# Convolution and attention on one core: queries of the last chunks on GpSimd, scores folded ahead of their copy, an earlier load of x

## The reference

```python
xf = x.reshape(b, c, n)
q = jnp.einsum('oc,bcn->bon', Wq, xf) + bq[None, :, None]      # 32 x 4096
k = jnp.einsum('oc,bcn->bon', Wk, xf) + bk[None, :, None]      # 32 x 4096
v = jnp.einsum('oc,bcn->bon', Wv, xf) + bv[None, :, None]      # 256 x 4096
att = jnp.einsum('bdi,bdj->bij', q, k) / jnp.sqrt(d_k)
att = jax.nn.softmax(att, axis=-1)
out = jnp.einsum('bcj,bij->bci', v, att).reshape(b, c, h, w)
cat = jnp.concatenate([gamma * out, x], axis=1)
fused = jnp.einsum('oc,bchw->bohw', Wf, cat) + bf[None, :, None, None]
```

## Time and profile before

| | us |
|---|---|
| median of 3 executions | 1976.79 (1976.61 to 1981.90) |
| the profiled execution, whole | 1979.12 |
| its span, first to last instruction | 1977.3 |
| TensorE busy | 1951.3 |
| VectorE, ScalarE, GpSimd busy | 1686.4, 1712.1, 1393.9 |
| mean granted clock of TensorE | 0.995 |

### The profile page before, as it was taken

The page is one execution under the profiler, slowest core; times in us unless marked ns, Lnnn a source line. Parts: engine busy times, 40 slices in busy tenths (PEclk is TensorE's granted clock), DMA queues, the critical chain, the costliest instruction groups (busy, mean ns, idle before and its releaser), DMA issues.

```text
span 1977.3 us, 46381 instructions
## 1 busy us (share of the span) xinstructions
PE 1951.3 (99%) x15656; PEld 1920.5 (97%) x15656; DVE 1686.4 (85%) x2713; ACT 1712.1 (87%) x2282; POOL 1393.9 (70%) x669
## 2 busy tenths in 40 slices
PE   9999999999999999999999999999999999999999
PEld 8899999999889999999988999999998899999998
DVE  7888888887788889988688888899868888888896
ACT  7799999997779999999778999999978899999996
POOL 3577777778457777777746777777765677777775
PEclk9999999999999999999999999999999999999999
DMA  4211111110321111111042111111104111111111
GB/s 147 80 19 19 18 21 21 21 18 16 123 72 23 17 17 20 21 21 22 12 129 67 23 22 16 18 19 21 22 12 134 38 23 22 21 16 17 20 22 17
DMA packets 297816, 69.70 MB, mean 35 GB/s; under 512 B 280528, under 2 KB 281296, under 8 KB 297680
## 3 DMA queue, kind: packets, MB, share of 16 engines
q1 hardware_dynamic: 296864, 67.90, 15.9%
q10 hardware_dynamic: 816, 0.13, 0.0%
HBM read 34.41 MB, written 33.55 MB: 34 GB/s over the span
## 4 chain that ended last, share of the span: by engine, by line
PE 93%; DVE 3%; issue 1%; DMA 1%; ACT 1%; SPq 1%; POOL 0%; DVEq 0%; ACTq 0%; POOLq 0%
PE ps_o L417 75%; PE ps_s L409 11%; PE ps_p L284 3%; PE ps_o L284 3%; PE ps_s L301 1%; DMA xf<-x 1%; DVE top L649 1%; PE ps_p L319 1%; PE ps_p L315 1%; SPq L154 1%; DVE kq_rest L749 0%; DVE kq_rest L742 0%; DVE keys L746 0%; ACT keys L507 0%; DVE lo L636 0%
## 5 line engine op out<-in xcount | busy, mean ns | idle before, releaser
L842 POOL TENSOR_TENSOR raw<-raw,top_m 128x1024 f32<-128x1024 f32 x508 | 1208.8, 2413 | 281.5 <-DVE top_m L684 244.4
L695 DVE TENSOR_TENSOR lo<-ps_p,hi 128x1024 fp32r<-128x1024 f32 x512 | 622.6, 1216 | 166.9 <-ACT ps_p L578 160.9
L649 DVE TENSOR_TENSOR top<-ps_s,top 128x512 f32<-128x512 f32 x960 | 658.5, 686 | 60.1 <-ACT raw L495 10.5
L417 PE MATMUL ps_o<-val_hi,hi 128*128 128x258 f32 x4096 | 663.7, 284 | 12.7 <-DVE val_lo L759 12.7
L571 ACT ACTIVATE hi<-raw 128x1024 fp32r<-128x1024 f32 x508 | 539.6, 1062 | 153.7 <-PE ps_o L417 143.3
L417 PE MATMUL ps_o<-val_lo,hi 128*128 128x256 f32 x4096 | 656.6, 282 | 0.0
L417 PE MATMUL ps_o<-val_hi,lo 128*128 128x258 f32 x4096 | 600.2, 284 | 0.0
L417 PEld LDWEIGHTS ps_o<-val_hi,hi 128*128 128x128 f32 x4096 | 566.7, 190 | 14.4 <-DVE val_lo L759 10.7
L495 ACT ACTIVATE raw<-ps_s 128x512 f32<-128x512 f32 x1024 | 552.7, 592 | 30.2 <-PE ps_s L409 2.7
L417 PEld LDWEIGHTS ps_o<-val_lo,hi 128*128 128x128 f32 x4096 | 563.7, 190 | 0.0
L417 PEld LDWEIGHTS ps_o<-val_hi,lo 128*128 128x128 f32 x4096 | 540.7, 191 | 0.0
(11 more groups left out here) (69 smaller groups left out, 1076.6 us busy)
## 6 DMA issues: line engine op xcount, KB each, us to landing
xf<-x SPq DMA_DIRECT2D x32, 512.0 KB, 3.9
conv_d<-conv_st SPq DMA_DIRECT2D x64, 256.0 KB, 2.0
result<-conv_d SPq DMA_DIRECT2D x512, 32.0 KB, 1.8
out<-result SPq DMA_DIRECT2D x510, 32.0 KB, 1.6
raw<-wf2T SPq DMA_DIRECT2D x1, 256.0 KB, 3.6
raw<-wv SPq DMA_DIRECT2D x1, 256.0 KB, 4.1
raw<-wf1T SPq DMA_DIRECT2D x1, 256.0 KB, 4.6
raw<-wkqT ACTq DMA_DIRECT2D x1, 64.0 KB, 2.6
```

What stands on the lines that cost most here:

```text
L417: last = nc.tensor.matmul(ps_o[:, i, 0:width], p[:, t % 2, jl * I + i * P:jl * I + (i + 1) * P], v[:, j, 0:width], start=opens and jl == 0 ...
L649: nc.vector.tensor_tensor(top[:, new], scores, top[:, new if half else old], ALU.max).then_inc(max_done, 1)
L695: nc.vector.tensor_tensor(lo[:, t % 2], ps_p[:].rearrange("p h n -> p (h n)"), hi[:, t % 2].bitcast(F32), ALU.subtract).then_inc(lo_done, 1)
L842: nc.gpsimd.tensor_tensor(raw[:, slot], raw[:, slot], top_m[:, r].unsqueeze(1).broadcast_to((P, JQ, I)), ALU.subtract).then_inc(sub_done, 1)
```

## The change

In chunks 6 and 7 (`LATE` is 6) the queries no longer go through VectorE. ScalarE copies rows 64 to 127 of `ps_p` with the bias, unrounded, into a new tile `q_raw` (the bias of rows 96 to 127 is set to zero for that); GpSimd rounds the queries out of it, copies them, and makes their rest with two operations of two inputs. Subtracting the split of x's chunk 7 goes from GpSimd to VectorE. TensorE waits for `q_raw` in place of the finished queries before it writes `ps_p[:, 0]` again, and for the queries themselves only in stage 2 of block 0.

For chunk 7's scores the order of ScalarE and VectorE is turned round: VectorE folds as soon as TensorE has written, and ScalarE copies once the fold is counted; ScalarE takes the second convolution of chunk 6 ahead of these copies. TensorE and GpSimd get a wait each for these copies in the first block, since the fold's count no longer implies the copy. In stage 0 of block 0 `scores_ahead` comes before `lead_first`.

The load of chunk 2 of the next image goes from the projection's start to just before the stores of the last block, behind a wait for the split of chunk 0.

```diff
@@ SyncE
-                    if c + 2 < CHUNKS:
+                    if c + 2 < CHUNKS and (c > 0 or first):
                         sp.wait_ge(x_split, b * CHUNKS + (c + 1))
                         load_x(b, c + 2)
                     store_conv(b, c)
@@ SyncE, attend_image
                 for n in range(BLOCKS):
+                    if not last_image and n == BLOCKS - 1:
+                        sp.wait_ge(x_split, b * CHUNKS + (CHUNKS + 1))
+                        load_x(b + 1, 2)
@@ TensorE, project
-                    pe.wait_ge(q_out, C + 1)
-                    pe.wait_ge(q_copied, C + 1)
+                    pe.wait_ge(q_raw_done, b * (CHUNKS - LATE) + (CHUNKS - LATE))
                     convolve(ps_p[:, 0], 0)
...
                 if c == CHUNKS - 2:
-                    pe.wait_ge(q_out, C + 1)
+                    pe.wait_ge(k_out, C + 1)
+                    pe.wait_ge(q_raw_done, b * (CHUNKS - LATE) + 1)
                     project_kq(c + 1, C + 1)
@@ TensorE, attend
                     a = t + AHEAD
+                    if first and t == 1:
+                        pe.wait_ge(raw_done, H + 2 * (a - 1))
...
+                    if first and t == 2:
+                        pe.wait_ge(q_out, b * CHUNKS + CHUNKS)
+                        pe.wait_ge(q_copied, b * CHUNKS + CHUNKS)
                     if first and t == 0:
+                        scores_ahead(t)
                         lead_first()
-                        scores_ahead(t)
@@ ScalarE
-                    act.wait_ge(s_ready, base + (2 * made + half + 1))
+                    act.wait_ge(max_done if folded else s_ready, base + (2 * made + half + 1))
...
-                    nc.scalar.activation(queries[2 * CK:R3, span(c)], ps_p[2 * CK:R3, 0], ACT.Identity,
-                                         bias=bkkqq[2 * CK:R3]).then_inc(q_hi_done, 1)
+                    if c < LATE:
+                        nc.scalar.activation(queries[2 * CK:R3, span(c)], ps_p[2 * CK:R3, 0], ACT.Identity,
+                                             bias=bkkqq[2 * CK:R3]).then_inc(q_hi_done, 1)
+                    else:
+                        act.wait_ge(q_out, C)
+                        nc.scalar.activation(q_raw[2 * CK:P], ps_p[2 * CK:P, 0], ACT.Identity,
+                                             bias=bkkqq[2 * CK:P]).then_inc(q_raw_done, 1)
...
                 if last_chunk:
+                    conv_out(ps_p[:, 1], 1, C - 1)
                     early_scores(c)
-                    conv_out(ps_p[:, 1], 1, C - 1)
@@ VectorE
-                    dve.wait_ge(raw_done, base + (h + 1))
+                    dve.wait_ge(s_ready if at_once else raw_done, base + (h + 1))
...
+                    if c >= LATE:
+                        return
+                    if c == 0 and not first:
+                        dve.wait_ge(q_out, C)
...
                 kq_lo(c, C)
+                if c == CHUNKS - 2:
+                    split_x(C + 1, c + 1)
@@ GpSimd, project
-                if c > 0:
+                if c == CHUNKS - 1:
+                    pool.wait_ge(q_out, C)
+                elif c > 0:
                     pool.wait_ge(x_split, C + 1)
...
+                    L = snap(pool, b * (CHUNKS - LATE) + (c - LATE))
+                    pool.wait_ge(k_copied, C + 1)
+                    pool.wait_ge(q_raw_done, L + 1)
+                    pool.sem_inc(kq_seen, 1)
+                    nc.gpsimd.tensor_copy(queries[2 * CK:R3, span(c)], q_raw[2 * CK:R3]).then_inc(q_rounded, 1)
+                    pool.wait_ge(q_rounded, L + 1)
+                    pool.sem_inc(kq_seen, 1)
+                    nc.gpsimd.tensor_copy(queries[0:CK, span(c)], queries[2 * CK:R3, span(c)]).then_inc(q_copied, 1)
+                    pool.wait_ge(q_copied, C + 1)
+                    pool.wait_ge(q_out, C)
+                    nc.gpsimd.tensor_tensor(kq_rest[R3:P], q_raw[2 * CK:R3], queries[2 * CK:R3, span(c)].bitcast(F32),
+                                            ALU.subtract).then_inc(q_rest_done, 1)
+                    pool.wait_ge(q_rest_done, C + 1)
+                    nc.gpsimd.tensor_tensor(queries[CK:2 * CK, span(c)], q_raw[R3:P], kq_rest[R3:P],
+                                            ALU.add).then_inc(q_out, 1)
@@ GpSimd, attend
+                    if t == QUADS - 3 and isinstance(n, int) and n == 0:
+                        pool.wait_ge(raw_done, b * HALVES + 2 * AHEAD)
```

More of the change, by code:

```diff
@@ L213, in store_last, with project_image @@
                         store_piece(sp, b, n, i, g)
-            def project_image(b):
+            def project_image(b, first):
                 for c in range(CHUNKS):
-                    if c + 2 < CHUNKS:
+                    if c + 2 < CHUNKS and (c > 0 or first):
                         sp.wait_ge(x_split, b * CHUNKS + (c + 1))
@@ L617, in spread_bkq @@
                 dve.wait_ge(vec_loaded, 16)
-                for g, u in enumerate((0, 0, 1, 1)):
-                    last = nc.vector.tensor_copy(bkkqq[g * CK:(g + 1) * CK], bkq[u * CK:(u + 1) * CK])
+                nc.vector.memset(bkkqq[R3:P], 0.0)
+                nc.vector.tensor_copy(bkkqq[0:CK], bkq[0:CK])
+                last = nc.vector.tensor_copy(bkkqq[2 * CK:R3], bkq[CK:2 * CK])
                 last.then_inc(bkq_spread, 1)
@@ L637, in split_x, with fold_scores @@
                                         ALU.subtract).then_inc(x_split, 1)
-            def fold_scores(base, made, old, new, halves=(0, 1)):
+            def fold_scores(base, made, old, new, halves=(0, 1), at_once=False):
                 for half in halves:
@@ L864, in project @@
                 nc.gpsimd.tensor_copy(keys[CK:2 * CK, span(c)], keys[0:CK, span(c)]).then_inc(k_copied, 1)
-                pool.wait_ge(q_hi_done, C + 1)
-                pool.wait_ge(k_copied, C + 1)
-                pool.sem_inc(kq_seen, 1)
-                nc.gpsimd.tensor_copy(queries[0:CK, span(c)], queries[2 * CK:R3, span(c)]).then_inc(q_copied, 1)
-                if c < CHUNKS - 1:
+                if c < LATE:
+                    pool.wait_ge(q_hi_done, b * LATE + (c + 1))
+                    pool.wait_ge(k_copied, C + 1)
+                    pool.sem_inc(kq_seen, 1)
+                    nc.gpsimd.tensor_copy(queries[0:CK, span(c)], queries[2 * CK:R3, span(c)]).then_inc(q_copied, 1)
                     pool.wait_ge(q_copied, C + 1)
```

22 lines of the change are left out of this document (15 added, 7 removed).

## The result

| | before | after |
|---|---|---|
| median | 1976.61 us (5 executions) | 1968.11 us (5, 1967.36 to 1968.25) |
| the profiled execution | 1979.12 | 1968.11 |
| its span | 1977.3 | 1966.3 |
| mean granted clock | 0.995 | 0.997 |

The ratio of the mean times is 0.9951, with an interval of 0.9936 to 0.9965; by the medians the change makes the kernel 8.5 us faster. Forecast were 1957 us and a range of 1953.5 to 1967.0; the time is 1.1 us outside the range, and the gain less than half of the 20 us forecast. So the question of this part is where the rest of the expected gain went.

The account below looks back on a forecast made before the run. TensorE was busy 99% of the span, so only its stands and slow-clock time could give: 17.1 us at the heads plus 3.0 for the load, 20.1, less 0.3 for the port, off 1976.79 gives 1957 us; range 1953.5 to 1967.0.

Parts of the forecast that it names:

- So at 1.3 us GpSimd costs nothing: Chunks 6 and 7: GpSimd's two-input operations take 1.3 us each and delay nothing; from 1.7 us they would.
- the chain: Start of chunk 7's projection to start of `lead_first`: forecast to shorten by 7.2 us over four images.
- rival E: Shared port: GpSimd work beside VectorE's two-input operations; a doubled split costs 3.2 us, 1960 us; chance 0.05.
- I take the clock as held: Head of the attention: TensorE stands 1.2 us instead of 3.13, so the clock stays at 1.00.
- rival A: Head of the attention: the clock falls anyway, total gain 14.3 us, 1962.5 us; chance 0.12.
- rival D: Stages 1 to 3: ScalarE and VectorE can't keep up at full clock, 1 us per image, 1961 us; chance 0.12.
- The load: x's chunk 2 loaded earlier: TensorE's projection wait goes in three images, taken as 3.0 us together.
- Folding ahead of the copy: Chunk 7: VectorE folds before ScalarE copies; costed at nothing, between a gain and a loss of 0.5 us.
- Stage 0 at the full clock: First stage of the attention: 24 matmuls, 2.9 us, plus a wait for `lo`, 3.4 us.
- The queries off the chain: Chunk 7: VectorE's 1.5 us of query work between the keys' rest and the folds goes.
- rival B: GpSimd sets the pace and the kernel is slower; 1984 us at 4 us per two-input operation; chance 0.04.
- C: Rival: the load gives nothing, as another input of chunk 1 is as late; 1960 us; chance 0.10.

Follow-up runs that it names:

- e2: The changed kernel with two more waits on GpSimd, keeping its two-input operations off VectorE's split and first maximum; 1967.75 us.
- e3: The changed kernel with a second buffer for raw queries, and GpSimd's copy of chunk 7's keys ahead of chunk 6's two operations; 1966.72 us.
- e11: e3 with chunk 7's two GpSimd operations put off behind the head, to stage 4 of block 0; 1964.48 us.
- e5: The changed kernel with GpSimd making only chunk 7's queries; chunk 6's stay on VectorE and chunk 7's split on GpSimd; 1965.10 us.
- e10: e5 with one more wait: GpSimd's stage 5 subtraction in block 0 starts only behind the second block's maximum; 1965.47 us.
- e4: The changed kernel with 12 unneeded score matmuls filling TensorE's stand ahead of `lead_first`; 1966.86 us.
- e6: The changed kernel with ScalarE's copies of chunk 7's scores ahead of the folds again and its last convolution's order put back; 1968.18 us.
- e1: The kernel before the change with only the earlier load of x's chunk 2; 1974.06 us.

## Why the prediction was wrong

The direction was right, with every part of the change doing what it says. The sum was 20.1 us against the profiled execution and 11.0 came. Three steps failed, and the baseline.

1. **"So at 1.3 us GpSimd costs nothing", and the folds from 554.85.** This is the step with the largest miss: the chain gained 2.3 us and not 7.2. The size of an operation by itself was right (1.28 to 1.29 us measured, 1.3 taken). What was wrong was to let it run beside VectorE: the first took 2.16 us, so chunk 6's queries were ready 2.72 us behind the start of the projection (547.87 to 550.59), where the forecast has 1.88 (551.47 to 553.35). ScalarE waited 0.95 us for them, the copy of the keys came behind them, and the folds began 4.10 us behind the projection, not 3.38 (0.72 lost). Then the maximum stood 0.58 us for GpSimd. Together 1.3 us per image, 5.2 in four; the table is short by 4.9. That was rival E, which I had given 0.05 and priced for the split only. Its evidence was read wrongly. The mean of 64 maxima, 435 ns against 420, was taken for the price of lying beside GpSimd. In that trace no maximum takes more than 0.49 us; those of 0.46 to 0.49 start when a subtraction of GpSimd has only 0.2 us left. The 15 ns are the price of such tails and say nothing about a maximum that starts with 0.7 us of the other's instruction left, as in after. e2 (the same operations at other times: 1719 to 1288 ns) and e3 (a copy of 0.16 us at 1.15) show the exclusion, e11 shows the chain without it (11.6 us). It also bears out what the Trainium skill says, in the page "SBUF — State Buffer", section "SBUF: two separate sides": the pair of ports that VectorE and GpSimd share is an exclusive lock, held for the whole instruction, and the other fully blocks. The traces agree in each meeting (2.16, 1.00 and 1.15 us above), but for 0.12 to 0.14 us: by that rule each would have been priced at the remainder of the other's instruction, 1.00, 0.71 and 1.13 us, where 0.88, 0.58 and 0.99 were lost.

2. **"I take the clock as held."** It fell in three of four images, at stands of 1.70, 1.66 and 2.17 us, and held in image 0 at one of 2.23. That was rival A, 0.12. Stage 0 gained 5.2 us and not 8.5. The stand was longer than the 1.2 us of the forecast mainly because of step 1 (the chain), so this miss is half a child of the first: in the profiled executions of e5 and e11, with a shorter chain, the clock held in all four images, in that of e10, with e5's chain, in three. But the rule used, that the length of the stand decides, is itself not one (last section).

3. **Nothing behind the head gives way (rival D, 0.12).** e4 holds the clock and gets 1.3 us for 3.6; e5, e10 and e11 gain 11.8 to 14.1 us up to stage 1 and keep 0.9 to 1.9 in the rest, where runs with a slow head keep 3.3 to 4.9. In after it is image 0, whose clock held, that gives 1.0 us back, as much as the whole shortfall of the rest. D looked for the loss in stages 1 to 3, in ScalarE and VectorE at their own pace. It came in stages 6 and 7 of the first block, and what was late there was VectorE, held up in the second block's maximum by GpSimd (the table under e4): step 1 once more, in a place that the prediction didn't look at. ScalarE's own pace is not it: it needs 2.85 us per stage (its exponentials start at 562.13 and 565.00 in e5) against TensorE's 3.36, and in image 1 of e4 and of e5 it has already waited 0.2 us for TensorE, twice, before it waits for VectorE. No run takes this meeting away altogether with the clock held in all images; where it is absent by chance (images 1 and 2 of e5), 0.2 us is lost, with a wait for `hi`.

4. **The baseline.** I took the sum made against a profiled execution of 1979.12 us off the median of 1976.79, 2.3 us below. But what the change removes here is in part time at the slow clock, of which that execution may have had more than the median one; after's profiled execution is at its median (1968.11), and the profiled gain is 11.0 us where the medians give 8.5. Taken off the profiled execution my own sum gives 1959.3, as the prediction said in brackets. The later runs of before bear that out: of 28 executions those with a mean granted clock of 0.996 to 0.998 took 1975.4 to 1978.5 us, those with 0.992 to 0.994 took 1979.2 to 1981.7. A median of before hangs on how many of each it has; against the 1979.68 us of one such set e6, as fast as after, is 11.5 us faster. So part of the shortfall against 20 us, 2 to 3 us of it, is luck of the executions and none of the mechanism.

5. **What held.** The load: forecast 3.0, measured 3.9 in e1 in the three stretches that it bears on, all three waits gone. Folding ahead of the copy: forecast at nothing, measured at 0.07 us. Stage 0 at the full clock: forecast 3.4, measured 3.41 in image 0 and 3.2 to 3.4 in e4. The queries off the chain: the step of 1.5 us per image is there (e11: 1.7 with the earlier end of the keys), once GpSimd is out of the way. GpSimd as the pace that makes the kernel slower (rival B) did not come.

The terms account for the difference: 4.87 (chain) + 3.26 (stage 0) + 1.01 (rest) = 9.1 us, which is 20.1 - 11.0; less the 0.3 that I had set aside for the port, and with 2.3 of the baseline, this is the 11.1 us between 1957.0 and 1968.11. As for the range: each of A, D and E was priced and given its chance as if it came alone. They came together, and they are not independent, since the port makes the stand, and the stand the slow clock; the range was reckoned from A with one other (by the prediction's own prices 1965.5 us with C and 1966.5 with D, where it says 1966 to 1967) and stopped 1.1 us short.

## What to carry to other kernels

Work moved off a busy engine to GpSimd was free here only where VectorE did not read SBUF with two inputs, or copy in it, at the same time: go through the timeline and, for each pair that overlaps, add what is left of the other's instruction. A group's mean prices only the meetings that the trace already has; look at the longest records and at how much of the other's instruction was left. And an earlier start moves meetings too, so look for new ones behind the place that was shortened. Price rivals that share a cause together, not one by one. Of the 6.5 us more that e11 gains up to stage 1, 2.5 are lost again behind it. Better than the change as made were half of it (1965.10) and the whole with the second half of its work behind the head (1964.48).

## What the runs showed of the hardware

**One waits for the whole instruction of the other.** Beside each other VectorE and GpSimd took: split of 128x1024, 1.45 us for 1.22 (beside a GpSimd copy); GpSimd's 32x512 with two inputs, 2.16 for 1.28; maximum of 128x256, 1.00 for 0.42; copy of 32x8, 1.15 for 0.16. In each case the instruction is longer by what was left of the other's instruction when the later one started (0.37, 1.00, 0.71 and 1.13 us), less 0.12 to 0.14 us. VectorE's instructions that read PSUM (the folds, 3.08 us for four in after and e3 alike) were not longer. GpSimd's operation costs the same on 32 partitions (1.28 us) as on 128 (1.295).

**The clock isn't decided by the length of one stand.** In e5 TensorE stood 0.77 us, made four scores, stood 0.50 us, and the clock stayed at 2.4 GHz. In e10, at the same place in image 2, it stood 0.73 and 0.53 us, and 1.3 us after the start of `lead_first` the clock fell to 1.2 GHz. TensorE's timeline and two windows of e10:

```profile
1045.44 0.73 PE L420 MATMUL ps_s<-queries,keys 96*128 96x256 f32 x4 [0.73 <-issue]
...
1046.70 0.51 PE L428 MATMUL ps_o<-val_hi,hi 128*128 128x258 f32 x2 [0.53 <-DVE val_lo L786]
...
1047.88 0.53 PE L428 MATMUL ps_o<-val_hi,hi 128*128 128x258 f32 x2
```

```profile
1047.00:1048.50 1.50, 1.50 (x12) 1.44 (x11) 1.09 (x2) 0.62 (x1) 1.50 (x1) 0.83 0.17 51
1048.50:1051.00 2.50, 2.50 (x14) 2.50 (x14) 0.38 (x1) 1.39 (x2) 2.50 (x3) 0.50 0.15 29
```

The stand of 2.23 us in image 0 of after did not bring it down. So a stand between 0.5 and 2.2 us may or may not cost some 1.1 us of slow clock (stage 0 at 4.4 to 4.6 us against 3.3). Filling it (e4) kept the clock in all four images, as did the shorter chain of e11; an estimate for a kernel with such stands needs both outcomes in its range.

**The way back of a loop.** The attention of images 1 and 2 begins in a new round of the engines' loop, that of images 0 and 3 doesn't. In e5 ScalarE's second exponential of the head started 3.33 us behind the start of GpSimd's first subtraction in image 1 (558.80 to 562.13, row above); that subtraction takes 2.40, so 0.93 us passed. In image 0 the idle time before that exponential is 1.02 us, in image 1 1.92, in image 2 1.93, in image 3 1.08. TensorE's scores ahead of the head have an idle time put down to its own issue of 0.61 us in image 1 and 0.77 in image 2, and none in the other two (70.29 and 1531.19). This is why stage 0 is 3.95 us in those images of e5 and 3.2 to 3.3 in the others. That it is the loop's jump is argued from where it comes, not tested.
